# Second cross attention of a six-stage model: probabilities turned by VectorE and DMA instead of TensorE, projection adds the heads

## What is computed

```
x = x + L1_xattn(layernorm(x), ctx_1024, ctx_1024, mask, ...)

Q = split_heads(x_q @ W_q.T + b_q)          # [B, 16, 32, 8]
K = split_heads(x_k @ W_k.T + b_k)          # [B, 16, 257, 8]
V = split_heads(x_v @ W_v.T + b_v)
scores = einsum('bhqd,bhkd->bhqk', Q, K) / sqrt(8)
scores = where(mask == 0, -1e9, scores)
attn = softmax(scores, axis=-1)
out = einsum('bhqk,bhkd->bhqd', attn, V)    # heads put side by side
return out @ W_o.T + b_o
```

## Time and profile before

| | |
|---|---|
| median of 3 runs | 2273.7 us (2273.0 to 2273.99) |
| span of the profiled execution | 2270.1 us |
| busy, share of the span: TensorE matmul / weight load | 86% / 68% |
| busy: VectorE, ScalarE, GpSimd | 72%, 72%, 40% |
| first and last exponential of the stage (`b_prob`) | 1334.1 and 1824.9 us |

### The profile page before, as it was taken

How to read it: one execution, slowest core, us unless ns; L and a number is a source line. 1 busy time by engine, 2 the same in 40 slices (tenths; PEclk the granted TensorE clock), 3 DMA queues, 4 the chain that set the end, 5 groups by cost and what they waited for, 6 DMA issues and landing times. The chain is left out here.

```text
span 2270.1 us, 55792 instructions
## 1 busy us (share of the span) xinstructions
PE 1957.3 (86%) x15563; PEld 1549.6 (68%) x15563; DVE 1626.0 (72%) x5153; ACT 1640.6 (72%) x4441; POOL 899.0 (40%) x1338
## 2 busy tenths in 40 slices
PE   3799999999999999995350579999999989858997
PEld 3688888888888888883240257777777756526775
DVE  5677777777777777764778758888888878854564
ACT  3588888888888888876486368888888878735553
POOL 1533443444433333422245123333333357533554
PEclk8699999999999999997585789999999999969999
DMA  4211111111110111100000022222222100013222
GB/s 134 73 34 34 33 33 33 33 33 33 29 28 27 30 33 33 33 4 1 0 0 0 0 73 66 74 65 65 74 65 65 52 2 0 1 28 84 89 83 84
DMA packets 124106, 93.89 MB, mean 41 GB/s; under 512 B 14417, under 2 KB 101937, under 8 KB 123905
## 3 DMA queue, kind: packets, MB, share of 16 engines
q1 hardware_dynamic: 122550, 90.88, 14.6%
q10 hardware_dynamic: 1194, 1.58, 0.2%
q0 software_dynamic: 288, 0.56, 0.1%
HBM read 88.26 MB, written 4.72 MB: 41 GB/s over the span
## 5 line engine op out<-in xcount | busy, mean ns | idle before, releaser
L750 ACT ACTIVATE a_prob<-a_neg,a_nmax 128x289 f32<-128x289 f32 x512 | 270.5, 530 | 79.0 <-DVE a_nmax L679 72.9
L1686 ACT ACTIVATE b_prob<-b_neg,b_nmax 128x257 f32<-128x257 f32 x512 | 255.2, 500 | 71.2 <-DVE b_nmax L1633 71.1
L645 POOL TENSOR_TENSOR a_xn<-a_z,g 128x256 f32<-128x256 f32 x128 | 93.3, 729 | 526.3 <-DVE a_z L705 526.3
L807 PE MATMUL a_score<-a_xnT,a_qT 128*128 128x290 f32 x1536 | 274.8, 315 | 1.1 <-DVE a_qT L726 1.1
L835 PE MATMUL a_out<-a_probT,a_xn 128*128 128x256 f32 x1024 | 263.6, 380 | 0.3 <-DVE a_probT L690 0.3
L679 DVE CUSTOM_DVE_ANT_0 a_neg<-a_score,a_bias 128x289 f32<-128x289 f32 x512 | 222.0, 459 | 46.4 <-PE a_score L807 40.0
L807 PEld LDWEIGHTS a_score<-a_xnT,a_qT 128*128 128x128 f32 x1536 | 216.5, 191 | 43.8 <-issue 43.2
L1633 DVE CUSTOM_DVE_ANT_0 b_neg<-b_score,b_bias 128x257 f32<-128x257 f32 x512 | 195.9, 421 | 50.8 <-PE b_score L1729 48.6
L755 ACT ACTIVATE a_prob<-a_prob,a_rinv 128x256 f32<-128x256 f32 x512 | 230.4, 499 | 1.1 <-DVE a_rinv L717 1.0
L835 PEld LDWEIGHTS a_out<-a_probT,a_xn 128*128 128x128 f32 x1024 | 175.0, 191 | 13.6 <-DVE a_probT L690 0.6
L1607 POOL TENSOR_TENSOR b_last_part<-b_v_rows,b_prob 128x128 f32<-128x128 f32 x128 | 52.0, 406 | 318.2 <-ACT b_prob L1686 318.2
(11 more groups left out here) (479 smaller groups left out, 5192.2 us busy)
## 6 DMA issues: line engine op xcount, KB each, us to landing
a_raw<-in_ctx SPq DMA_DIRECT2D x128, 128.0 KB, 3.4
b_raw<-in_ctx SPq DMA_DIRECT2D x128, 128.0 KB, 3.3
m_wide<-expert_weights SPq DMA_DIRECT2D x128, 128.0 KB, 2.9
a_kept<-keep SPq DMA_DIRECT2D x32, 257.0 KB, 3.9
b_kept<-keep SPq DMA_DIRECT2D x32, 257.0 KB, 3.5
b_v_rows<-ctx_tail_values SPq DMA_DIRECT2D x32, 256.0 KB, 3.6
a_tail<-latents_normalised SPq DMA_DIRECT2D x64, 64.0 KB
latents_normalised<-lat_affine SPq DMA_DIRECT2D x8, 256.0 KB, 2.3
```

The costliest lines, as they stand in the source:

```text
L750: nc.scalar.activation(prob[:, par, grp, :], neg[:, grp, :], ACT.Exp, bias=nmax[:, par, grp:grp + 1], scale=-1.0, accum_out=rsum[:, par, g ...
L807: last = nc.tensor.matmul(score_ps[grp % 2][:, 0:even(KEYS0)], qT[:, a, un, bn, 4 * grp:4 * grp + 4, :], xnT[:, c, n, :], start=(p == 0), ...
L1686: nc.scalar.activation(prob[:, n, grp, :], neg[:, par, grp, :], ACT.Exp, bias=nmax[:, par, grp:grp + 1], scale=-1.0, accum_out=rsum[:, n, ...
```

## The change

In words: TensorE no longer turns `prob`. VectorE transposes the first 256 columns of the four groups in one instruction over 1024 columns (`turn_blocks`), which turns every 32x32 block in place, for the batch one ahead of the step; four DMAs from SBUF to SBUF (`spread_prob`), one per 32 partitions, put the blocks where the matmul wants them. For this the keys are computed in another order (a permuted output of the keys' product), and the mask is stored in that order (`key_order`). The four masking instructions now stand together behind the transpose, three batches ahead instead of two. The key bias is added by ScalarE in the keys' copy, and the mask acts through `bias` alone; `kT` gets the tail's column from a `k_tail` that is projected once ahead. The sum over the four heads is no VectorE instruction any more: four accumulating matmuls of the projection do it. The value bias is folded into `bo` ahead of the loop. Keys and values have a bank each, the projection's output lies in the free columns of the last score bank. Input is turned five batches ahead, keys and values four.

```diff
+def key_order(cols, kt):
+    return cols.rearrange("p (j t c) -> p t c j", j=KEY_STEP, t=2)[:, kt]
...
-                nc.vector.tensor_scalar(m1b[:], m1[:], 0.0, None, ALU.not_equal).then_inc(mask_ready, 1)
+                for kt in range(2):
+                    nc.vector.tensor_scalar(key_order(m1b[:, 0:2 * P], kt), m1[:, kt * P:(kt + 1) * P].rearrange("b (c j) -> b c j", j=KEY_STEP),
+                                            0.0, None, ALU.not_equal)
+                nc.vector.tensor_scalar(m1b[:, 2 * P:N_CTX], m1[:, 2 * P:N_CTX], 0.0, None, ALU.not_equal).then_inc(mask_ready, 1)
...
+                    dve.wait_ge(bv_done, 1)
+                    nc.vector.tensor_tensor(k.bo[:], bv_ps[:], k.bo[:], ALU.add).then_inc(bo_ready, 1)
+                    dve.wait_ge(k_done, 1)
+                    nc.vector.tensor_scalar(k_tail[:], tail_ps[:], k.bk1, None, ALU.add).then_inc(k_copied, 1)
...
-        kT = sb("b_kT", [P, 4, N_CTX])
+        kT = sb("b_kT", [P, 8, N_CTX])
-        probT = sb("b_probT", [P, 2, CH])
+        blocks, probT = sb("b_blocks", [P, 2, N_BLOCKS, GROUPS, L]), sb("b_probT", [P, 2, 4, 2, GROUPS, L])
-        turn_ps = [psum("b_turn0"), psum("b_turn1")]
+        k_ps, v_ps = psum("b_k"), psum("b_v_ps")
-        proj_ps = out_ps[:, P:2 * P]
+        proj_ps = score_ps[GROUPS - 1][:, 3 * P:4 * P]
-        LEAD, LAG = 5, 2
+        LEAD, LAG, TURN = 5, 1, 1
...
+                def spread_prob(g, j):
+                    s, n = g * 8 + j, (j + TURN) % 2
+                    sp.wait_ge(blocks_ready, s + TURN + 1)
+                    wait(sp, out_ready, s + TURN - 1)
+                    for i in range(4):
+                        sp.dma_start(probT[:, n, i].rearrange("p t g l -> p (t g l)"),
+                                     blocks[i * L:(i + 1) * L, n].rearrange("c (r t) g l -> c r (t g l)", t=2)).then_inc(probT_loaded[n], 16)
...
+                    if live(g, j, TURN):
+                        spread_prob(g, j)
...
+                def keys(t, u, loads):
+                    slots = slice(4 * u, 4 * u + 4)
+                    nc.gpsimd.tensor_copy(kT[:, slots, N_CTX - 1:N_CTX], k_tail[:, ds(t * BPT, BPT)].unsqueeze(2))
+                    wait_apart(k, pool, kept_loaded[u], loads * 16)
+                    nc.gpsimd.tensor_scalar(bias[:, slots, :], kept[:, u], NEG0, -NEG0, ALU.mult, ALU.add).then_inc(keys_ready, 1)
...
+                def turn_blocks(g, j):
+                    s, n = g * 8 + j, (j + TURN) % 2
+                    dve.wait_ge(exped, (s + TURN + 1) * 4)
+                    if live(g, j, TURN - 2):
+                        dve.wait_ge(probT_loaded[n], probT_loads(g, j + TURN - 2))
+                    nc.vector.transpose(blocks[:, n].rearrange("p r g l -> p g r l"),
+                                        prob[:, (j + TURN) % 4, :, 0:2 * P].rearrange("p g (r c) -> p g r c", c=L)).then_inc(blocks_ready, 1)
...
-                        dve.wait_ge(turned[0], s + 1)
-                        nc.vector.tensor_copy(probT[:, 0, :], turn_ps[0][:]).then_inc(probT_ready[0], 1)
+                    if live(g, j, -1):
+                        dve.wait_ge(out_ready, s)
+                        dve.wait_ge(in_copied, s + 5)
+                        if b == 1:
+                            wait(dve, proj_ready, t - 1)
+                        nc.vector.tensor_tensor(own[:, (j - 1) // 4 % 2, :, (j - 1) % 4, :], out_ps[:, 0:P].rearrange("p (h l) -> p h l", l=L),
+                                                turned_in[:, (j + 4) % 8, W0:W0 + P].rearrange("p (h l) -> p h l", l=L),
+                                                ALU.mult).then_inc(own_ready, 1)
                     if live(g, j, 1):
                         n = (j + 1) % 4
                         dve.wait_ge(exped, s * 4 + 8)
                         wait(dve, weight_ready, s - 2)
                         nc.vector.reciprocal(rinv[:, n, :], rsum[:, n, :]).then_inc(rinv_ready, 1)
+                    if live(g, j, TURN):
+                        turn_blocks(g, j)
+                    if live(g, j, 3):
+                        for grp in range(GROUPS):
+                            mask(g, j, grp)
                     if b == 0 and live(g, j, -1):
-                        nc.vector.tensor_reduce(oT_sum[:], own[:].rearrange("p b h l -> p b l h"), AX.X, ALU.add).then_inc(sum_ready, 1)
...
-                        nc.vector.scalar_tensor_tensor(kT[:, n, :], turn_ps[0][:, 0:N_CTX], k.bk1, kept[:, (j + 3) // 4 % 2, n, :],
-                                                       ALU.add, ALU.mult).then_inc(k_ready, 1)
...
-                        nc.scalar.activation(probT[:, 1, :], turn_ps[1][:], ACT.Copy).then_inc(probT_ready[1], 1)
...
+                        nc.scalar.activation(kT[:, (j + 4) % 8, 0:2 * P], k_ps[:, 0:2 * P], ACT.Identity, bias=k.bk1).then_inc(k_ready, 1)
...
+                    copy_keys(g, j)
+                    copy_values(g, j)
+                    exps(g, j, range(GROUPS))
...
-                def turn(g, j, kt):
-                    for grp in range(GROUPS):
-                        last = nc.tensor.transpose(turn_ps[kt][:, grp * P:(grp + 1) * P],
-                                                   prob[:, j % 4, grp, kt * P:(kt + 1) * P], k.ident[:])
-                    last.then_inc(turned[kt], 1)
...
+                    if kt == 0:
+                        pe.wait_ge(probT_loaded[j % 2], probT_loads(g, j))
...
+                    if live(g, j, 3):
+                        score(g, j)
+                    if b == 0 and live(g, j, -1):
+                        pe.wait_ge(own_ready, s)
+                        for h in range(HG):
+                            last = nc.tensor.matmul(proj_ps, own[:, 1 - u, h].rearrange("p b l -> p (b l)"), k.wo1[:],
+                                                    start=(h == 0), stop=(h == HG - 1))
+                        last.then_inc(proj_ready, 1)
...
+                        nc.tensor.matmul(k_ps[:, 0:2 * P].rearrange("p (j t c) -> p t c j", j=KEY_STEP, t=2), k.wk1[:], turned_in[:, n, C0:C0 + 2 * P],
+                                         start=True, stop=True).then_inc(k_done, 1)
```

More of the change, by code:

```diff
@@ L1709, in step @@
-                    if live(g, j, 2):
-                        exp(g, j, 2)
-                        exp(g, j, 3)
-                    if b == 0 and live(g, j, -1):
-                        act.wait_ge(sum_ready, t)
-                        wait(act, proj_ready, t - 1)
-                        nc.scalar.activation(oT[:], oT_sum[:], ACT.Identity, bias=k.bv1).then_inc(oT_ready, 1)
+                        end = C0 + 2 * P if live(g, j, 5) else C0
+                        act.wait_ge(in_turned, s + 6)
@@ L1717, in _ @@
+                        nc.scalar.activation(turned_in[:, (j + 5) % 8, first:end], in_ps[:, first:end], ACT.Copy).then_inc(in_copied, 1)
+                    copy_keys(g, j)
+                    copy_values(g, j)
+                    exps(g, j, range(GROUPS))
                 run_steps(act, step, LEAD, LAG)
@@ L1748, in step @@
                     s, t, u, b = g * 8 + j, tile_of(g, j), j // 4, j % 4
-                    here, ahead = live(g, j, 0), live(g, j, 4)
-                    if here:
-                        pe.wait_ge(exped, s * 4 + 4)
-                        pe.wait_ge(k_ready, upto(g, s, 3))
-                        turn(g, j, 0)
-                        pe.wait_ge(v_ready, upto(g, s, 3))
-                        turn(g, j, 1)
-                    if here or ahead:
-                        wait(pe, in_copied, s + 4)
+                    here, ahead = live(g, j, 0), live(g, j, 5)
+                    if live(g, j, 3):
+                        score(g, j)
[5 more added lines that the diff above has]
+                        last.then_inc(proj_ready, 1)
+                    if here or ahead:
+                        wait(pe, in_copied, s + 5)
+                        if ahead:
+                            n = (j + 5) % 8
+                            pe.wait_ge(raw_loaded[n], (g + (j + 5) // 8 + 1) * 16)
+                            for kt in range(2):
+                                last = nc.tensor.transpose(in_ps[:, C0 + kt * P:C0 + (kt + 1) * P], raw[:, n, kt, :], k.ident[:])
                         if here:
@@ L1760, in step @@
                             last = nc.tensor.transpose(in_ps[:, W0:W0 + P], weight[:, j % 2], k.ident[:])
-                        if ahead:
-                            n = (j + 4) % 8
-                            pe.wait_ge(raw_loaded[n], (g + (j + 4) // 8 + 1) * 16)
-                            for kt in range(2):
-                                last = nc.tensor.transpose(in_ps[:, C0 + kt * P:C0 + (kt + 1) * P], raw[:, n, kt, :], k.ident[:])
-                        last.then_inc(in_turned, 1)
@@ L1781, in step @@
+                    if live(g, j, 4):
+                        n = (j + 4) % 8
+                        wait(pe, v_ready, s + 4)
                         for kt in range(2):
```

(2 more changed lines are left out.)

184 lines of the change are left out of this document (77 added, 107 removed).

## The result

| | before | after |
|---|---|---|
| median of 7 runs | 2273.7 us | 2282.23 us (2278.73 to 2287.24) |
| ratio, 95% interval | | 1.004 [1.0029, 1.0051] |
| span of the profiled execution | 2270.1 us | 2278.1 us |
| period of the batch loop | 3.85 us | 3.86 us |

The forecast was 2241 us and faster. The time lies inside the range of 2213 to 2318, on the wrong side of before.

What follows compares the result with a forecast made beforehand. TensorE was taken to set the pace at 3.85 us a batch; a period of 3.55 over 127 intervals saves 38 us, less 5 for the end, giving 2241 us, with a range of 2213 to 2318.

Steps and rivals of the forecast that it cites:

- Steps 1 and 2: TensorE loses the transposes of prob, its projection adds the four heads: 4.05 us with projection, mean 3.23 a batch.
- Step 3: VectorE loses 1.43 us of work a batch and gains a 1024-column transpose of 1.20; busy 3.0 us.
- Rival B: VectorE's transpose runs at the strided rate, 2.1 us in place of 1.2; slower, 2323 us; chance 0.07.
- Step 4: ScalarE loses a probT copy and takes the keys' copy with bias: 3.2 us, no cost while the period is above.
- Step 5: Hand-overs: one step at TensorE's 4.05 plus 0.2, three at VectorE's 3.1 plus 0.1; floor 3.46 us a batch.
- Step 6: SP issues four spreading DMAs a batch, 2.6 us of issues in all; two-batch loop gives (T + 2.6)/2 = 3.5 us.
- T: The spread's transfer time: three issues of 0.47 us, then the last one's landing; taken as 4.4 us.
- DMA engines: Throughput with the spread added: 2.7 to 3.1 us needed of a 3.5 us period, nearly full; 0.1 added for lumps.
- Step 8: After the last exponentials, three steps instead of two with the transfer exposed: 5 us more, between 0 and 8.
- Rival A: The spread transfer bounds, each DMA reading only 32 partitions: 4.4 us a batch, 2349 us; chance 0.18 including milder forms.
- Rival C: The keys' product on TensorE is slowed by its strided PSUM output: no gain, 2272 to 2283 us; chance 0.10.
- D's: The rival that hand-overs cost nothing and the DMA hides: period 3.34 us, faster, 2214 us; chance 0.14.

Runs made afterwards that it cites:

- the swap: The changed kernel with VectorE turning the next batch's blocks before working out own instead of after it; 2257.6 us, 0.9927 of before.
- the wide one: The changed kernel with its four transfers a batch each reading 1 KB from all 128 partitions instead of 4 KB from 32; 2256.4 us.
- two ahead: Against the best kernel (transpose before own, three transfers on SP, one on GpSimd, four slots), each step turns the batch after next; 2458.6 us.
- two queues: The changed kernel with two of the four spreading transfers of a batch issued by GpSimd instead of SP; 2299.0 us, 1.011 of before.

## Why the prediction was wrong, step by step

- **What bounds before**: right as far as it goes. Without the spread (3.23 us) TensorE's relief gives 3.85 - 3.23 = 0.62 us a batch, and the time falls by 82.
- **Steps 1 and 2**, TensorE: right. The eight projection instructions take 1.16 us (forecast 1.10).
- **Step 3**, the transpose: 1.245 us against 1.20; VectorE 81 of 100, or 3.1 us a batch against 3.0. Rival B is out.
- **Step 4**, ScalarE: 82.6/26 = 3.2 us as said.
- **Step 5**, the floor: 3.46 forecast, 3.23 measured. I put one TensorE step and three VectorE steps behind each other with gaps between. The means that I had for the single engines (TensorE 3.23, VectorE 3.27, ScalarE 3.2) were nearer, and without the spread ScalarE is busy 95 of 100 us and VectorE 93, so the long step and the hand-overs cost next to nothing. How the queues hide them was not followed. An error of 0.23, hidden by the next.
- **Step 6**, the spread: here it failed, twice. *An issue* was put at 0.47 us from two loads at the loop's start; a spread issue takes 0.60 by its record, and 0.62 to 0.63 with the gap to the next of the four. *SP's whole* was put at 2.6 us, "and fits"; it measures 3.69: four issues at 0.62 and the loads, plus 0.2 us between any two groups of them, which I left out. That sentence closed off the queue as a bound, when it was the larger one. T was put at 4.4; it measured 1587.18 - 1581.80 = 5.38 in the loop shown and 5.01 in the next. Of the first one's excess of 0.98, 0.70 are the loads in front and 3 x 0.63 - 1.4 = 0.49 the length of the issues, less 0.2 for a landing that is a little faster than I had it. In the next the issues began 0.18 after the blocks, and their length is most of the excess of 0.61. What remains of the loop, 2.4 us, came out as forecast (2.6). By the prediction's own formula, (5.2 + 2.4)/2 = 3.8.
- **DMA engines**: forecast a need of 2.7 to 3.1 us a batch; measured 0.771 x 200/52 = 2.97. Not the bound, as the swap shows.
- **Step 8**, the end: 5 us forecast, 6.8 measured, inside 0 to 8. Four value products wait 1.1 to 2.2 us each for a transfer. TensorE, busy 0.68 of the 2 us from 1824, runs at the lower level of its clock (0.50) from about 1827. A stretch and the last product of the timeline:

```profile
1834.00:1838.00 4.00, 2.49 (x23) 1.43 (x21) 0.58 (x2) 0.28 (x1) 0.00 (x0) 0.50 0.30 75
1835.99 1.08 PE L1774 MATMUL b_out<-b_probT,b_v 128*32 128x128 f32 x16 [1.08 <-DMA b_probT<-b_blocks]
```

  A product of 0.65 us takes 1.08, and the projection 2.07 instead of 1.16. Before, the clock was 1.00 until 1832, past the last projection.

- **Rival A** named T = 5.0 as the point from which the change is slower; T was 5.2, and slower it was. Its reason was half right. The narrow source costs real DMA time (267 GB/s against 341 for the wide one), yet at equal issues going wide brings just 0.17 us, since SP's queue then holds the loop. It was the issue length and the queue that carried T over the point. **Rival C** is out. **D's** 3.34 was above the true floor.
- **The chances**: the case that came true, a period from 3.81 on by SP's issue time, had no line of its own.

## What to carry to other kernels

An issue of a DMA is work of the engine that issues it: count every issue of a step with its own duration and the gap behind it, add them up as for any engine, and compare the sum with the period. For a transfer inside a dependency loop ask how many batches the loop spans. Moving one VectorE instruction ahead of a wait made it three instead of two and turned a loss of 8 us into a gain of 16, but turning one batch further ahead closed a loop through ScalarE and cost 249 against the same kernel without it. And an edit that relieves the second bound shows nothing, or the wrong sign, until the first is gone.

## What the runs showed of the hardware beside that

- A 128 KB transfer inside SBUF, with runs of 1 KB, takes SP 0.60 us to issue by the median record, from 32 partitions as from 128 (0.47 for 512 KB from 128 in runs of 4 KB, 0.37 to 0.46 for a raw load from HBM in the change). GpSimd's took 0.57 to 0.58, no more than SP's, but landed after 3.5 to 3.7 us against 2.9 to 3.3 for SP's in the same runs, with the DMA engines 78 to 87% busy. With them 58% busy (two ahead) it was 3.0 against 2.9. Waiting for the blocks, GpSimd began its issue 0.63 us after them in the median (two queues), SP 0.02.
- A 512 KB copy inside SBUF from all partitions landed after 3.2 us, 1.0 later than one of 128 KB from all partitions; the same read out of 32 partitions, 6.2.
- VectorE's transpose of 1024 f32 columns takes 1.245 us, hardly more than a 1024-column reduction (1.205).
